# A two-layer cross-attention kernel with its queues ordered operation by operation, and its query stacks turned by DMA transposes

## The reference, cut to what matters

```python
x = x + xattn0(layernorm(x), ctx, ctx, mask0)      # 16 heads of 8, a mask for each sequence
x = x + bitffn(layernorm(x))                       # gate, up, down with ternary weights
x = x + xattn1(layernorm(x), ctx, ctx, mask1)      # 16 heads of 8, one shared mask
x = x + moe(layernorm(x))                          # 8 experts, top 2 of them weighted

# attention:   q, k, v = x @ Wq.T, ctx @ Wk.T, ctx @ Wv.T   (split in 16 heads of 8)
#              softmax(where(mask == 0, -big, q k^T) * scale) @ v, then @ Wo.T
# bitffn:      act_quant(x) = round(x * 127/max|x|) / (127/max|x|), weights rounded to -1, 0, 1
#              down( act_quant( silu(gate(x)) * up(x) ) )
# moe:         top 2 of x @ Wg.T + bg, softmax of the two;  relu(x W1 + b1) W2 + b2, weighted sum
```

## Time and profile before

| | us |
|---|---|
| median of 3 runs (lowest to highest) | 238.72 (238.11 to 239.03) |
| the profiled execution | 239.16 |
| its span in the trace | 237.3 |
| PE busy, share of the span | 201.5, 85% |
| DVE busy | 169.5, 71% |
| ACT busy | 134.3, 57% |
| POOL busy | 110.6, 47% |
| loads from device memory, all issued at the start | 5.80 MB |

### The profile page before, as it was taken

How to read it: one execution, slowest core, us unless ns; L and a number is a source line. 1 busy time by engine, 2 the same in 40 slices (tenths; PEclk the granted TensorE clock), 3 DMA queues, 4 the chain that set the end, 5 groups by cost and what they waited for, 6 DMA issues and landing times.

```text
span 237.3 us, 5951 instructions
## 1 busy us (share of the span) xinstructions
PE 201.5 (85%) x2097; PEld 166.0 (70%) x2114; DVE 169.5 (71%) x573; ACT 134.3 (57%) x377; POOL 110.6 (47%) x232
## 2 busy tenths in 40 slices
PE   0467299988675799898999999999899999999993
PEld 0245077866353577675779789897779979999992
DVE  1541974899999999999888998679756364625335
ACT  2242028685445465585959666567567738366560
POOL 6997022352475746423244562845262460482531
PEclk9999999999999689999999999999999999999998
DMA  6999044244003147040404002340400400000000
GB/s 203 356 397 201 1 88 41 53 90 91 0 3 62 28 88 91 0 91 15 82 0 76 15 4 38 64 91 11 91 0 3 91 12 4 0 14 11 14 0 22
DMA packets 39442, 15.09 MB, mean 64 GB/s; under 512 B 34163, under 2 KB 38515, under 8 KB 39158
## 3 DMA queue, kind: packets, MB, share of 16 engines
q1 hardware_dynamic: 38982, 14.00, 27.3%
q10 hardware_dynamic: 432, 0.72, 0.9%
HBM read 5.80 MB, written 0.52 MB: 27 GB/s over the span
## 4 chain that ended last, share of the span: by engine, by line
PE 49%; DVE 33%; DMA 4%; issue 4%; POOL 4%; SPq 2%; ACT 2%; DVEq 0%; ACTq 0%; POOLq 0%; another core or an unknown queue 0%
PE ps_B L705 11%; PE ps_A L720 10%; DVE mx L924 7%; PE ps_O L648 4%; PE ps_A L591 4%; PE ps_A L593 3%; PE ps_Q L637 3%; PE ps_B L606 3%; PE ps_B L608 3%; DMA wf_sb<-in_wd 3%; PE ps_P L628 2%; POOL yc L553 2%; DMA kblk<-kst 2%; DVE z L988 2%; PE ps_O L657 2%
## 5 line engine op out<-in xcount | busy, mean ns | idle before, releaser
L924 DVE TENSOR_REDUCE mx<-ps_A 128x4 f32<-128x512 f32 x64 | 41.9, 681 | 10.0 <-PE ps_A L593 9.5
L806 ACT ACTIVATE probs<-ps_B 128x512 f32<-128x512 f32 x64 | 36.9, 608 | 12.3 <-PE ps_B L608 11.9
L816 ACT ACTIVATE hid<-ps_B,b_sb 128x128 f32<-128x128 f32 x128 | 35.6, 383 | 12.7 <-PE ps_B L705 12.6
L591 PE MATMUL ps_A<-m_b,id_b 128*128 128x512 bf16 x64 | 25.9, 405 | 11.7 <-DVE mx L924 8.8
L705 PE MATMUL ps_B<-mxT,w_sb 128*128 128x128 f32 x256 | 33.5, 279 | 0.1
L720 PE MATMUL ps_A<-w_sb,hid 128*128 128x128 f32 x256 | 31.1, 275 | 0.4
L720 PEld LDWEIGHTS ps_A<-w_sb,hid 128*128 128x128 f32 x256 | 31.1, 192 | 0.6
L705 PEld LDWEIGHTS ps_B<-mxT,w_sb 128*128 128x128 f32 x256 | 30.6, 192 | 0.3 <-issue 0.2
L443 POOL TENSOR_SCALAR hv<-mv 128x1 f32<-128x1 f32 x32 | 7.3, 229 | 50.3 <-DVE mv L899 50.2
L553 POOL TENSOR_TENSOR yc<-yc 128x512 f32<-128x512 f32 (+2 forms) x21 | 17.2, 818 | 27.0 <-DVE yc L1052 25.9
L452 POOL TENSOR_SCALAR xh<-x_sb,mv,ry 128x128 f32<-128x128 f32 x32 | 26.1, 816 | 3.5
(11 more groups left out here) (128 smaller groups left out, 399.8 us busy)
## 6 DMA issues: line engine op xcount, KB each, us to landing
w_sb<-in_m1T SPq DMA_DIRECT2D x1, 1024.0 KB
w_sb<-in_m2T SPq DMA_DIRECT2D x1, 1024.0 KB
ctx_sb<-in_ctxT ACTq DMA_DIRECT2D x1, 512.0 KB, 5.0
m_i<-in_mask SPq DMA_DIRECT2D x1, 512.0 KB, 6.8
m0T_i<-in_mask0T SPq DMA_DIRECT2D x1, 512.0 KB, 7.5
out_y<-out_sb SPq DMA_DIRECT2D x8, 64.0 KB, 1.6
x_sb<-in_x SPq DMA_DIRECT2D x1, 448.0 KB, 5.5
wf_sb<-in_wg SPq DMA_DIRECT2D x1, 256.0 KB, 6.0
```

Of the source, the lines that this page charges most:

```text
L591: pe.matmul(o[:, :].rearrange("p (h k) -> p h k", h=4), id_b[:, :], m, start=True, stop=False)
L806: ins = act.activation(probs[:, n % 2, 4 * i:4 * i + 4, :], psum("exp", n, i)[:, :].rearrange("p (h k) -> p h k", h=4), ACT.Exp, scale=ATT ...
L816: ins = act.activation(hid[:, b % 2, 4 * i + c, :], psum("z", b, i)[:, c * P:(c + 1) * P], ACT.Relu, bias=b1_sb[:, 4 * i + c:4 * i + c + 1])
L924: ins = dve.tensor_reduce(mx[:, n % 2, 4 * i:4 * i + 4], psum("max", n, i)[:, :].rearrange("p (h k) -> p h k", h=4), AX.X, ALU.max)
```

## The change

- The steps of the plan are single operations now, on DVE and POOL above all: "dve.parts" became m1, mr, m2, m3; the FFN's quantising became q0, qa, qi, qc, xr, xq and h0 to h3, hr, hq; the bias splitting is five steps of its own, the rounding of the weights nine, the weights' sums three. m2 is taken from the maxima themselves, no longer copied from the rest. Each step has a semaphore of its own (`done`), and a step waits for those it needs (`after`).
- The plan's table `TIME` holds two numbers a step, how long it keeps its engine and when its result is there. `START`, `BIAS` and UNIT_ORDER have new values (sequence 7 of layer 0 comes one place later).
- Keys and values are a step ("kv", bank X) of their own, apart from the query ("q", bank P, which now has two slots), and don't wait for the layer norm. Bank Q is gone.
- Both turns of the query stack are DMA transposes on SP's queue, behind and between those of the keys. PE's 8 transposes and ACT's copy are gone both times.
- The normalising itself (x minus mean, times the inverse root) moved from POOL to DVE (steps nm and fn); POOL keeps the inverse root.
- Loads: the context and the weights of the first unit come first, with semaphores of their own; the small bias is loaded ahead of the expert weights.

```diff
-BANK = {"max": "A", "gate": "A", "up": "A", "y": "A", "exp": "B", "z": "B", "xT": "P", "qkv": "P", "fxT": "P",
-        "mxT": "P", "qb": "Q", "qs": "Q", "pv": "O", "oT": "O", "aT": "O", "wo": "O",
-        "hT": "X", "down": "X", "logit": "X"}
...
+BANK = {"max": "A", "gate": "A", "up": "A", "y": "A", "exp": "B", "z": "B", "xT": "P", "q": "P", "fxT": "P",
+        "mxT": "P", "kv": "X", "hT": "X", "down": "X", "logit": "X", "wm": "X",
+        "pv": "O", "oT": "O", "aT": "O", "wo": "O"}
+RING = {"A": 2, "B": 2, "P": 2, "X": 1, "O": 1}
...
-    ("dve.parts", 1, "dve.max"),
-    ("pe.qb", 1, "dve.parts"),
-    ("act.qb", 1, "pe.qb"),
-    ("pe.exp", 4, "act.qb"),
...
+    ("dve.m1", 1, "dve.max"),
+    ("dve.mr", 1, "dve.m1"),
+    ("dve.m2", 1, "dve.m1"),
+    ("dve.m3", 1, "dve.mr", "dve.m2"),
+    ("sp.qb", 1, "dve.m3"),
+    ("pe.exp", 4, "sp.qb"),
...
+                if name == "qs":
+                    after(sp, "pool.ql", n)
+                    if n >= 2:
+                        after(sp, "pe.max", n - 2)
+                        wait_landed(sp, n - 2, "qs")
+                    sp.dma_start_transpose(qT[:, n % 2, :, :], qst[:, n % 3, :, :].rearrange("p g c -> p (g c)")
+                                           ).then_inc(landed["qs"][n % 2], 16)
+                if name == "qb":
+                    after(sp, "dve.m3", n)
+                    if n >= 2:
+                        after(sp, "pe.exp", n - 2)
+                        wait_landed(sp, n - 2, "qb")
+                    sp.dma_start_transpose(qmT[:, n % 2, :, :], qst[:, n % 3, :, :].rearrange("p g c -> p (g c)")
+                                           ).then_inc(landed["qb"][n % 2], 16)
...
-            def stack(name, n, src, rows):
...
-                for g in range(GROUPS):
-                    mm = pe.transpose(o[0:rows, g * P:(g + 1) * P], src[:, g, 0:rows], id_b[:, :])
...
-                    if (l, b) == (0, 1): ternary_weights()
-                    if (l, b) == (1, 0): bias_parts()
...
+                if name == "nm":
+                    after(dve, "pool.pw", n)
+                    if n >= 2:
+                        after(dve, "pe.xT", n - 2)
+                    ends(dve.tensor_scalar(xh[:, n % 2, :], x_sb[:, b, :], mv[:, 2 * l, b, 0:1], ry[:, 2 * l, b, :],
+                                           ALU.subtract, ALU.mult), "dve.nm")
```

More of the change, by code:

```diff
@@ L130 @@
 )
[L132 to L146, removed]
-)
@@ L149 @@
[L149 to L157, removed]
@@ L261, in build, with place @@
     units, order = UNIT_ORDER, plan()
-    number = {unit: n for n, unit in enumerate(units)}
-    count, where = {}, {}
+    counts = {s[0]: s[1] for steps in STEPS for s in ONCE + steps}
+    in_attention = {s[0] for s in ATTENTION}
+    def place(name, n):
+        return n if name in in_attention else units[n][1] if name not in {s[0] for s in ONCE} else 0
+    fills, before = {}, {}
     for name, n, i in order["pe"]:
-        bank = BANK[name]
-        u = units[n][1] if name in PER_BATCH else n
-        where[name, u, i] = (bank, count.get(bank, 0))
-        count[bank] = count.get(bank, 0) + 1
+        bank = fills.setdefault(BANK[name], [])
+        before[name, place("pe." + name, n), i] = (
+            len(bank) % RING[BANK[name]], bank[-RING[BANK[name]]] if len(bank) >= RING[BANK[name]] else None)
+        bank.append((name, place("pe." + name, n), i))
     with ExitStack() as ctx:
@@ new lines, in _ @@
+                if name == "max": maxima_scores(n, i)
+                if name == "exp": shifted_scores(n, i)
+                if name == "pv":
+                    after(pe, "act.v", n)
+                    after(pe, "act.exp", n)
+                    wait_free(pe, "pv", n)
+                    if n == 0:
+                        pe.wait_ge(bank_zero, 1)
+                    o = psum("pv", n)
+                    for h in range(H):
+                        j = h % 4
+                        mm = pe.matmul(o[32 * j:32 * j + DH + 1, (h // 4) * P:(h // 4 + 1) * P],
+                                       v_sb[:, n % KSLOTS, h, :], probs[:, n % 2, h, :], start=True, stop=True)
+                    ends(mm, "pe.pv")
@@ new lines, in _ @@
+                if name == "oT":
+                    after(pe, "act.pv", n)
+                    wait_free(pe, "oT", n)
+                    o = psum("oT", n)
+                    for g in range(4):
+                        mm = pe.transpose(o[:, g * P:(g + 1) * P], oT_sb[:, n % 2, g * P:(g + 1) * P], ident)
+                    ends(mm, "pe.oT")
+                if name == "aT":
+                    after(pe, "dve.at", n)
+                    turn("aT", n, attn[:, n % 2, :, :].rearrange("p h d -> p (h d)"), ident)
@@ new lines, in _ @@
+                if name == "z":
+                    if b == 0 and i == 0:
+                        pe.wait_ge(s_moe, 80)
+                    if i == 0:
+                        after(pe, "act.mxT", b)
+                    wait_free(pe, "z", b, i)
+                    for c in range(4):
+                        mm = pe.matmul(psum("z", b, i)[:, c * P:(c + 1) * P], w1_sb[:, 4 * i + c, :], mxT[:, b % 2, :],
+                                       start=True, stop=True)
+                    ends(mm, "pe.z")
@@ L1048, in weigh @@
[L1048 to L1055 removed]
+            last = [0]
```

1340 lines of the change are left out of this document (714 added, 626 removed).

## The result

The changed kernel takes 223.44 us (median; 222.18 to 223.78) against 238.88 us of the kernel before: 0.935 of its time, 95% interval 0.931 to 0.939, a gain of 15.4 us. The forecast was 216 (203 to 231), a gain of 22.8: the direction held and the size was 7.4 us too large. Times in this document are medians of all executions, while a ratio leaves out the slow ones (over 1.5% above the fastest of the same kernel), of which two kernels have one in four each: the last one, and the kernel after with its bias steps in DVE's gap, whose trace is of the slow one.

The account below looks back on a forecast made before the run. Bound by DVE from 45 to 120 us with PE close behind, then by PE; neither full in the head. Stacks -5.0, once-only -6.0, DVE -8.8, balance -4.0, landings +1.0 gave -22.8: 216 us, range 203 to 231.

Parts of the forecast that it names:

- Stacks and their landings: Query stacks leave PE for DMA: 11 stacks behind 120 us save 5.0 us, later landings cost 1 us.
- The cover that was named: Two or three units in flight and other work in PE's queue hide later landings; without it 59 us.
- The condition set for "right": Sign on PE: waiting for query stacks, plain and shifted, totals less than 3 us.
- Once-only work: Bias splitting leaves DVE's full middle, weight rounding moves from the head: 6 of 10 us saved, bounds 0 and -12.
- PE's stand of 4.83 us goes: Head: PE's wait before 28.42 us, behind the rounding of the weights, disappears.
- about 40% will still come where DVE is wanted: Discount on bias splitting and weight rounding, 10 us of DVE, leaving 6 us counted as saved.
- DVE's queue: Middle, 45 to 120 us: interleaved single operations remove waits, -11.4, normalising adds 2.6; sum -8.8 us.
- The +2.6 us for the normalising steps: Middle stage: 13 normalising steps come from POOL to DVE at 0.20 us each.
- Balance: PE, idle 12.1 us in the middle, pulls last-stage work forward: -4 us (0 to -6).
- the same 5.80 MB of loads: Head: it doesn't start sooner, since the first key stack is still behind these loads.
- the landings: Rival: PE stands before "max" or "exp" for late DMA stacks; at 0.9 us each, 244 us; chance 0.10.
- waits cost DVE what they did: Rival: reordering DVE's queue saves no waits, normalising +2.6, balance -2; 229 us (223 to 235), chance 0.13.

Follow-up runs that it names:

- the last one: Kernel after with expert weights ahead of the sixth unit's shifted query stack, bias row loaded ahead of the masks and five bias steps spread over the head: 217.03 us, 0.905.
- its control: Kernel after with one PSUM bank instead of two for query projections and input transposes, stacks still DMA transposes, queue order nearly kept: 227.06 us, 0.951.
- the 123 waits: Kernel after with every fourth VectorE step waiting for the end of the step before it in the queue, some 123 added waits: 232.17 us, 0.969.

## Why the forecast was right in direction and too large

*Stacks and their landings* (-5.0 + 1.0 = -4.0): right. Putting the stacks back costs 4.6 us with the landings in it. The cover that was named held: outside the head PE waited under 5 us for landings. The condition set for "right", under 3 us in all, was missed, since 7.8 us of the 12.5 fall in the head; but there the key transpose is late too, and the kernel with PE stacks starts its maxima only 0.9 us sooner than its control.

*Once-only work* (-6.0): this is the step that failed, in "the first 'exp' needn't wait for 34.95 us" and "PE's stand of 4.83 us goes". The condition for it was named (it falls if the first "exp" comes after 37 us) and it came at 38.08: by its own test the forecast falls, and the time still lies in its range because of the other terms. PE's stand before the second pair of maxima was replaced by one of 3.96 us before the next unit's. The bias steps were a gain of 3.5 us where they left and a loss of 2.8 us where they went: 0.7 us net of a term of 6. The forecast knew that they would delay the first unit by up to 3.3 us, and hid that in "about 40% will still come where DVE is wanted". Moving the rounding of the weights alone wasn't tried. In the kernel after it takes 41.51 to 45.62 us of DVE, just ahead of the full stage rather than in it, and PE's longest wait from 41 to 50 us is 1.08 us; what that is worth no run prices.

*DVE's queue* (-8.8): near the measured price in sum, by two errors that cancel, which is luck. The waits were sized by 0.11 us and 85%; measured are 0.12 us and 55%, and 8.1 us for about the same number of waits (spread over the whole run, while the forecast took those of the middle). The +2.6 us for the normalising steps doesn't show: taking them off DVE again gives nothing. It counted DVE's side alone and left out that the step is shorter there than on POOL.

Its signs were there: DVE's busy time is 161.6 us (155 to 170 was named), independent steps start 0.10 us apart, and in the middle DVE stands 1.2 us for maxima of PE. They tell little by themselves: with the 123 waits put in, DVE's busy time is 169.4 us, still inside, and independent steps started 0.09 us apart before the change too.

*Balance* (-4.0): part of it has a cause. The second bank for the front steps is worth 3.6 us, which the forecast didn't name as such. The rest of that term isn't separated from it.

The measured prices add to 4.6 + 0.7 + 8.1 + 3.6 = 17.0 us against 15.4; each is priced with the others in place, so they needn't add, the rounding of the weights has no price among them, and the 1.6 us aren't attributed further. Of the 7.4 us that were forecast too much, 5.3 would be the once-only term if the rounding was worth nothing where it went; what is left is of the size of these overlaps.

What was not seen is what the head had to offer. The forecast took the first key transpose as tied to "the same 5.80 MB of loads". It is tied to their order: 2 MB of them are first used at 108 us, and letting them go into a gap of SP's queue gives 5.0 us.

Of the rivals, the landings didn't decide: outside the head PE waits 4.7 us for them, where that rival needs 0.7 us at each of 32 places. The rival "waits cost DVE what they did" can't be excluded by the time, since 223.44 us lies on its edge (223 to 235) and not inside the forecast's likeliest case (209 to 223). What speaks against it is the run with waits put in: each costs DVE 0.12 us, and 8.1 us of them reach the end.

## What to carry to other kernels

A once-only piece of work that leaves a full stage isn't saved until the place where it goes is priced in the same way: read which engine stands there, and who waits behind it. In an in-order queue that carries loads and transposes together, a load costs what is queued behind it: put it directly ahead of an entry at which the queue already stands, since one entry later cost 6.0 us here (224.13 against 218.11). And 14 us of work taken from an engine that is 85% busy were worth under 5; the rest became idle time.

## What the runs showed of the hardware

- One instruction that turns a stack of 8 blocks lands in 3.3 to 3.5 us and one of 16 blocks in 5.1 us (medians), while SP is held 1.23 us for a stack; behind 2 MB of loads the first key transpose held SP for 7.43 us, without them it was 3.4 to 4.4 us.
- A wait of DVE for its own previous step costs 0.12 us, read from two pairs of steps.
- POOL took 2.3 to 3.0 us for a multiply or an add on 3 partitions of 1,024 numbers with F32 results, where DVE took 1.27 us for the multiply and the add together.
